# Attention step of a one-core Trainium2 kernel: the scores stand at the end of TensorE's step, the eight transposes of a step in one group

## The reference, cut to what matters

```python
# x: 2 x 2048 x 256 float32, 16 heads of 16
n = layernorm(x)
K = n.reshape(B, L, H, d)
Q = rms_norm_multihead((n @ Wq.T).reshape(B, L, H, d), q_norm_w)
V = rms_norm_multihead((n @ Wv.T).reshape(B, L, H, d), v_norm_w)
W = jnp.cumsum(jnp.einsum('blhd,blhe->blhde', K, V), axis=1)   # a running sum over the positions
x = x + jnp.einsum('blhd,blhde->blhe', Q, W).reshape(B, L, D)
# then on layernorm(x): 32 experts, top 4 of a softmax router, each silu(x W1) * (x W3) W2,
# plus a shared expert of the same form; x = x + y + z
```

## Time and profile before

| | us |
|---|---|
| median of 3 runs | 561.97 (561.77 to 563.79) |
| the profiled execution | 559.33 |
| its span, first to last instruction | 557.4 |
| around the span | 1.93 |
| stage of 31 attention steps with QV, first to last QV | 10.35 to 200.37 |

### The profile page before, as it was taken

The page is one execution under the profiler, slowest core; times in us unless marked ns, Lnnn a source line. Parts: engine busy times, 40 slices in busy tenths (PEclk is TensorE's granted clock), DMA queues, the critical chain, the costliest instruction groups (busy, mean ns, idle before and its releaser), DMA issues.

```text
span 557.4 us, 18176 instructions
## 1 busy us (share of the span) xinstructions
PE 527.4 (95%) x5177; PEld 383.1 (69%) x5177; DVE 382.2 (69%) x1354; ACT 376.5 (68%) x1258; POOL 331.8 (60%) x367
## 2 busy tenths in 40 slices
PE   6798999999999999699999999999999999997996
PEld 2355666666666665357998988999999995544554
DVE  7698999999999996664444444444444446744786
ACT  2687899988989985402766766777677776653452
POOL 6010377776777777771665555666666564446992
PEclk8999999999999999899999999999999999998999
DMA  8998355556456554954676776766666554428999
GB/s 259 316 292 264 125 217 211 187 215 227 186 198 246 188 192 152 366 194 127 195 219 201 221 225 199 214 193 194 194 193 198 180 187 145 143 79 342 408 409 347
DMA packets 65088, 123.29 MB, mean 221 GB/s; under 512 B 9824, under 2 KB 44000, under 8 KB 64992
## 3 DMA queue, kind: packets, MB, share of 16 engines
q1 hardware_dynamic: 47824, 78.07, 44.1%
q0 software_dynamic: 13056, 39.86, 19.2%
q10 hardware_dynamic: 4112, 4.19, 2.3%
HBM read 58.49 MB, written 63.60 MB: 219 GB/s over the span
## 4 chain that ended last, share of the span: by engine, by line
PE 79%; DMA 5%; DVE 4%; issue 4%; ACT 3%; POOL 2%; SPq 1%; ACTq 1%; DVEq 0%; POOLq 0%
PE pS L967 18%; PE pQV L828 10%; PE pS L985 9%; PE pS L741 8%; PE pS L795 5%; PE pO L888 5%; DMA xg<-xs 3%; PE pO L869 3%; PE pT L946 3%; PE pQV L946 2%; PE pQV L757 2%; PE pO L757 2%; PE pT L774 2%; PE pO L803 2%; PE pT L817 1%
## 5 line engine op out<-in xcount | busy, mean ns | idle before, releaser
L495 POOL DMA_INDIRECT ys<-gsh,dst x144 | 138.1, 959 | 108.3 <-ACT gsh L663 86.6
L467 POOL DMA_INDIRECT xs<-xg,posi x128 | 123.8, 967 | 52.1 <-issue 31.4
L967 PE MATMUL pS<-after_a,x2T_all 128*128 128x128 f32 x1024 | 135.5, 276 | 0.0
L967 PEld LDWEIGHTS pS<-after_a,x2T_all 128*128 128x128 f32 x1024 | 124.5, 192 | 0.0
L1375 DVE TENSOR_TENSOR after_a<-after_a,pS 128x128 f32<-128x128 f32 x144 | 41.5, 288 | 79.9 <-ACT after_a L651 76.1
L1346 DVE COPY x2T_all<-w 128x512 f32 x144 | 63.9, 444 | 32.9 <-issue 32.5
L985 PE MATMUL pS<-w,after_a 128*128 x256 | 76.7, 381 | 0.0
L1089 DVE TENSOR_TENSOR w<-pS,tri 128x512 f32<-128x512 f32 x96 | 65.1, 679 | 1.0 <-PE pS L795 1.0
L828 PE MATMUL pQV<-w 128*128 128x512 f32 x128 | 63.7, 621 | 0.5 <-ACT w L533 0.5
L663 ACT ACTIVATE gsh<-pS,xg 128x256 f32<-128x256 f32 x128 | 60.6, 474 | 0.4 <-issue 0.4
L662 ACT CAST dst<-xg 128x1 int32 x128 | 24.5, 191 | 45.3 <-PE pS L985 43.3
(11 more groups left out here) (221 smaller groups left out, 1019.8 us busy)
## 6 DMA issues: line engine op xcount, KB each, us to landing
xg<-xs SPq DMA_DIRECT2D x128, 160.0 KB, 2.8
ys<-gsh SPq DMA_DIRECT2D x32, 512.0 KB
w<-ys SPq DMA_DIRECT2D x32, 512.0 KB, 15.3
w<-in_L_ffn_W ACTq DMA_DIRECT2D x1, 4096.0 KB, 18.6
out<-xall SPq DMA_DIRECT2D x14, 256.0 KB, 7.2
xs<-padrow SPq DMA_DIRECT2D x32, 80.0 KB
xg<-xs SPq DMA_DIRECT2D x32, 80.0 KB, 2.2
ys<-gsh,dst POOLq DMA_INDIRECT x144
```

The lines of the kernel that those rows point to most:

```text
L467: pool.indirect_dma_start(out=xs, out_offset=bass.IndirectOffsetOnAxis(ap=posi[:, a.r8, k:k + 1], axis=0), in_=xr[:, a.r8, :], in_offset=N ...
L495: pool.indirect_dma_start(out=ys, out_offset=bass.IndirectOffsetOnAxis(ap=dst[:, j % 8:j % 8 + 1], axis=0), in_=y[:, j % 8, :], in_offset= ...
L967: last = pe.matmul(pS[a.b][:, n * P:(n + 1) * P], w13_staged(a.t)[:, (2 * k + n) * F:(2 * k + n + 1) * F], xgT[:, a.b, k, :], start=(k == ...
```

## The change

In PE's step the block of the scores is taken from between xnT and oT and put behind o2, at the end of the step, and there it handles tile i-1, not tile i-2. Its waits stay the same in form (`qm_done` of its tile, `masked` and `s_copied` of the tile before it). No other engine's order is changed. x2T, xnT, oT and qT, eight transposes, now follow each other.

```diff
@@ PE's step
                     last.then_inc(S["xnT_ps"], 1)
-                if (a := tile_of(2)) is not None:
-                    if a.t == 0:
-                        pe.wait_ge(S["consts_dve"], DVE_CONSTS)
-                    wait(pe, S["qm_done"], a.t + 1)
-                    wait(pe, S["masked"], banks_masked(a.t))
-                    wait(pe, S["s_copied"], banks_copied(a.t))
-                    for g in range(KC):
-                        for j in range(4):
-                            last = pe.matmul(pS[j][:, g * 256:(g + 1) * 256], xnT[32 * j:32 * j + 32, a.r3, g, :],
-                                             qm[32 * j:32 * j + 32, :, g, :], start=(g == 0), stop=True,
-                                             skip_group_check=True)
-                            if g == KC - 1:
-                                last.then_inc(S["scores_ps"], 1)
                 if (a := tile_of(3)) is not None:
                     wait(pe, S["oT_done"], a.t + 1)
...
                     last.then_inc(S["o_ps"], 1)
+                if (a := tile_of(1)) is not None:
+                    if a.t == 0:
+                        pe.wait_ge(S["consts_dve"], DVE_CONSTS)
+                    wait(pe, S["qm_done"], a.t + 1)
+                    wait(pe, S["masked"], banks_masked(a.t))
+                    wait(pe, S["s_copied"], banks_copied(a.t))
+                    for g in range(KC):
+                        for j in range(4):
+                            last = pe.matmul(pS[j][:, g * 256:(g + 1) * 256], xnT[32 * j:32 * j + 32, a.r3, g, :],
+                                             qm[32 * j:32 * j + 32, :, g, :], start=(g == 0), stop=True,
+                                             skip_group_check=True)
+                            if g == KC - 1:
+                                last.then_inc(S["scores_ps"], 1)
             pipelined(NT, 7, step)
```

## The result

The changed kernel takes 573.58 us in the median (572.86 to 574.68, 4 runs) against 562.36 (561.77 to 563.79, 4 runs) for the kernel before: a ratio of 1.0197, 95% interval 1.0171 to 1.0224. It is slower by 11.2 us. Forecast were 575.0 us, a ratio of 1.023, and a range of 570 to 582. One of the ten executions of the old order with Q's transposes in a bank of their own took 2919.86 us and is left out of its ratio.

What follows compares the result with a forecast made beforehand. PE was taken to bound the attention at 6.11 us per step. Losses of 12.8 (27 x 0.475), 0.4 and about 0.3 us, together 13.5, less perhaps 0.5 swallowed, gave +13.0: 561.97 becomes 575.0 us, range 570 to 582.

Steps and rivals of the forecast that it cites:

- The step that carries the forecast: Between xnT and qT on PE: without the scores, 0.77 us per step is a new wait for ACT's copies.
- The removed change of array mode: On PE, one change fewer between whole-array and 32-row matmuls around the scores: 0.12 us per step given back.
- POOL's wait of 0.21: Before o2 in step A, a wait for POOL's mask, expected to go: -0.20 us for two steps.
- step A: Attention step beginning with xnT at 149.45, alternating with step B; xnT to QV 2.00 us, expected to lengthen by 0.52.
- Terms left at nothing: Small waits in step B from QV to the rank product: taken as nothing, at most 0.17 us per pair.
- step B: Attention step beginning at 155.33, alternating with step A; xnT to QV 1.89 us, expected to lengthen by 0.63.
- 0.5 that is swallowed: Some steps between 40 and 75 us, already longer than 6.2 us, can swallow perhaps 0.5 us of the loss.
- signs of being wrong: L533 starting much sooner than 0.42 us after xnT, L817 before L539's end, or a shorter stage behind the attention.
- So PE sets the pace: Attention stage: PE busy 12.19 of 12.22 us for two steps, so it sets 6.11 us per step.
- The wait is not there: faster: Rival: copies come in time before qT, only the removed mode change counts; -0.39 us per two steps, 556 us, chance 0.05.
- More is lost: Rival: POOL's wait before o2 stays and o2 into scores costs 0.1 more; +0.2 per step, 581 us, chance 0.15.
- The same: Rival: time lost in the attention stage is won back behind it; 562 us, chance 0.05.

Runs made afterwards that it cites:

- work put into the hole: Changed kernel with one whole-array product of 256 columns between oT and qT in 27 steps: 571.41 us, ratio 1.0226; two steps 13.23.
- a longer copy: Changed kernel with ACT's copy of x2T made twice, the first into an unused buffer: 580.96 us, ratio 1.038; two steps 13.77.
- without the wait: Changed order with Q's transposes in the upper half of pT1, carried state spoilt: 562.85 us, ratio 1.0066; two steps 12.52.
- double exponential: ACT's exponential of the norm's root made twice: in the kernel before 562.17 us, ratio 1.0051; in the changed kernel 573.38 us, ratio 1.0245.
- early mask: Kernel before with POOL's mask between its first and second indirect DMA: 559.25 us, ratio 0.9976; two steps 12.23.

## Why the prediction was right, point by point

**The mechanism.** The step that carries the forecast, that the scores cover two ACT copies and that the copies stand in the open once the scores are gone, held. It is shown by three kinds of run: work put into the hole is free, a longer copy goes into every step in full, and without the wait most of the loss is gone. The prediction had everything on PE queued behind qT alone; in fact ACT's copy of qT, not QV, sets when the router's products and o1 start. That adds a little (below), and it is why the run with oT behind qT lost nothing up to o1.

**Its size.** From xnT to QV 1.44 us were summed, 1.41 are measured. Its links: copy 0.42 us after xnT's start (158.47 to 158.89), next copy 0.27 later, 0.38 long, then 0.10 to the first qT transpose and 0.24 to QV. o2 to the scores was taken as o2 to x2T, about 1.0, and is 0.99. The scores are 1.08 to the next group in both. The removed change of array mode was put at 0.12 us per step; xnT to its successor fell from 0.31 to 0.22 and oT to its successor from 0.27 to 0.22 (read where a product follows it without a wait), together 0.14. The drain that the Trainium skill, "TensorEngine Tiling (Array Packing)", section Key Properties, states is thus in the rows; it is worth less than a fifth of the cover that was given up for it.

**What loosened.** POOL's wait of 0.21 in step A went, as expected. Terms left at nothing were not nothing: QV to the router's product went from 1.79 to 1.86 us in step A (159.88 to 161.74), from there to o1 from 0.28 to 0.34, and QV to the router's product in step B from 1.96 to 2.00. These products wait for ACT's copy of qT, and ACT's queue behind the late copies is as tight as PE's. Two steps were put at 13.17 and take 13.23.

**The count.** From the first QV to the last the profiled executions give 190.0 us before (10.35 to 200.35, the table of the kernel before has 200.37) and 202.3 after (10.51 to 212.83): +12.3 for the 31 steps, where 12.7 were forecast (12.8 and 0.4, less 0.5 that is swallowed). Three of its terms were off and nearly cancel, which is luck. The windows of the two kernels, each over the eight steps from the fifth QV on and the 19 steps behind them, first before, then after:

```profile
33.99:84.17 50.18, 48.13 (x772) 31.21 (x771) 46.52 (x181) 43.59 (x144) 17.57 (x21) 1.00 0.65 218
84.17:200.35 116.18, 115.97 (x1868) 75.90 (x1867) 112.64 (x484) 105.58 (x360) 85.16 (x96) 1.00 0.56 207
```

```profile
35.07:87.00 51.93, 47.18 (x773) 30.64 (x772) 47.00 (x182) 43.45 (x144) 18.16 (x22) 1.00 0.62 208
87.00:212.83 125.83, 113.95 (x1868) 74.20 (x1867) 114.77 (x484) 106.04 (x360) 84.93 (x95) 1.00 0.51 190
```

The 19 regular steps lost 9.65 us, 0.51 each, against 0.475 forecast. The eight uneven steps lost 1.75 us, where eight times 0.51 would be 4.1: the stalls swallowed 2.3 us and not 0.5. The first four steps lost 0.9 (23.6 to 24.6 us) and not 0.4. The last two figures are of two single executions: the changed kernel with one product in the hole, whose regular steps are the same, took 25.8 us for the first four steps, and needed 203.6 from the first QV to the last. Behind the last QV the way to the first expert product takes 60.74 us before and 59.49 after, and 59.4 to 62.1 in the other runs; the experts themselves take 230.8 and 233.2, and 228.8 to 233.6 in the others. No part of the change can be told there. By its letter one of the prediction's signs of being wrong has come, a shorter stage behind the attention; the 1.25 us lie inside the spread of the other runs. The two profiled executions thus differ by 13.5 us (559.33 and 572.86) and the medians by 11.2; the 13.0 forecast lie between, and a difference of 2.3 us is within the spread of single executions.

**What bounds the kernel before.** "So PE sets the pace" was half of it. The double exponential and the early mask show a second bound at the same 12.2 us: in step A the ring from QV by way of the square, the root and the normalised V to the next QV, in step B ACT's copies, which stand behind the root's operations in ACT's queue. The prediction took step A's 2.00 us from xnT to QV, against 1.89 in B, as PE's work; 0.12 of it is the wait for V. It saw that Q was nearly as late as the copies, and not that the ring was a bound of its own. For the forecast it made no difference: in the changed kernel the double exponential leaves the regular steps at 13.23. It matters for the rivals.

**The rivals.** "The wait is not there: faster", 556 us, falls twice. The wait is there; and with the wait taken away the changed order is still at 1.0066 of the kernel before. Its sum of -0.39 for two steps took all PE time saved as time won. "More is lost" had two parts, POOL's wait staying and a dearer way from o2 into the scores; neither came. "The same" did not occur.

## What to carry to other kernels

Before grouping like operations of one engine, ask what the operation that is moved away was hiding. Here 0.14 us of changing array mode were saved and 0.75 us of cover for two copies were lost. When PSUM is full and a bank is written, copied out and written again within one step, the work between the two writes is not free to move.

A stage in which one engine is busy for 99% by its rows can have a second bound just behind. Adding a little work off that engine, or removing a small wait and seeing where it comes back, tells it in one run, if one reads which wait grew: an operation added to a queue pushes back everything behind it. A change of order that costs time need not cost it where the order was changed; moving oT lost nothing up to o1, and 0.21 us in two steps by way of DVE's masks.

## What the runs showed of the hardware that was not expected

The releaser column understates a wait behind transposes. Two transposes are 0.11 us apart from start to start, but the row of one is 0.27 us long; the hole that the column puts at 0.56 us took in 0.75 us of work.

An operation of DVE can stand until one of POOL has ended. DVE's small addition L1118, of two f16 tensors in SBUF, takes 0.16 to 0.18 us in every step of both kernels between 80 and 200 us, where it does not meet POOL's mask (L482). With oT behind qT it met the mask in ten steps from 88 us on, took 0.51 to 0.76 us and ended 0.04 us behind the mask's end each time; with the double exponential in the changed kernel it did so in four steps, with 0.96 to 1.06 us. DVE's L1089, in f32 and with one operand in PSUM, kept its length: 0.66 to 0.70 us for the 19 that met the mask in the kernel before between 80 and 200 us, as for the others. Whether the type or the place of the operands makes the difference, no run tells.

The stage's early steps are uneven in every run, in other places each time (one step of 7.1 us before, at 39.7; one of 7.4 at the very start after). In this pair of executions a new regular wait partly disappears in eight of them: 0.22 us per step in place of 0.51.
